# Waits of TensorE in the first attention, and the order of work in the mixture's front

## The chip, the cores and the metric

One core of a Trainium2 chip runs the whole program as one launch. Its engines work side by side and meet at semaphores: TensorE (PE, with its weight loads as PEld) multiplies, VectorE (DVE) and ScalarE (ACT) work on rows in SBUF and PSUM, GpSimd (POOL) and SyncE (SP) mostly issue transfers. The metric is the device time of one execution in microseconds, as the median of several runs. Before the change it is 1716.51 us (three runs, 1713.88 to 1717.43).

## What is computed

Two layers on 16 batches of 112 tokens of 256 features (1792 tokens), with a context of 375 rows for each batch:

```python
x = x + tanh(g_xattn[0]) * L0_xattn(layernorm(x), ctx)   # 16 heads of 64
x = x + tanh(g_ffn[0]) * L0_ffn(layernorm(x))            # quantised gate, up, down
x = x + tanh(g_xattn[1]) * L1_xattn(layernorm(x), ctx)   # 16 heads of 16, mask
x = x + tanh(g_ffn[1]) * L1_ffn(layernorm(x))            # mixture
# L1_ffn
normed = h * rsqrt(mean(h * h) + 1e-8) * norm_weight
shared = relu(normed @ sw1 + sb1) @ sw2 + sb2
probs = sigmoid(normed @ router_w.T)                     # 8 experts, the best 2
y = shared + sum over the 2 experts of weight * (relu(normed @ ew1 + eb1) @ ew2 + eb2)
```

## The kernel before

The kernel is written engine by engine: each phase is a block with one stream of instructions for each engine, in the order in which the Python code issues them, and `wait_ge(semaphore, value)` holds an engine's stream until a counter has reached a value. A block ends when all engines have reached its end. Every fp32 operand is split into a high and a low half in fp16, and a product is three matmuls (`products`, lines 294 to 296): ScalarE writes the high half, VectorE subtracts it and writes the low half.

**First attention** (`attention0_phase`). A slot g is one pair of heads of one batch; 8 slots are a batch, 128 slots in all. In slot g TensorE computes the scores of g (L505), the transposes of the probabilities of g-1 (L515), the first job of the slot, the weighted values of g-2 (to `a_ps_o`), and the rest of the jobs. Jobs are projections that later slots need: K, Q and V of a batch, the transposed output OT and the output product W. Their order is the table `JOBS`; `NUMBER` gives the place of a job in that sequence, and VectorE counts finished jobs in `job_lo`. A job may start when the job two places before it is finished (two PSUM banks), so that TensorE has by then waited for every value of `job_lo` up to that. ScalarE counts exponentials in `exp_done`, VectorE the low halves of the transposed probabilities in `pt_lo`, and the normalised outputs in `o_ready`. `scores(g)` waits for `job_lo` and for both exponentials of g-1; `transposes(g-1)` then waits again for those exponentials, one by one.

**Second attention** (`attention1_phase`) has slots of the same kind. In its last four slots (128 to 131) VectorE has only the last normalisation (`normalise`), the low half of the output (L1325) and the addition of W to the residual (L1333), each waiting for TensorE or ScalarE. SyncE stores each batch's residual to `out` (`kept`), the last one at L1127. After that block `clear_semaphores` runs, a short block of its own.

**The mixture's front** (`moe_front_phase`) begins with the statistics of the 16 batches (L1762, 16 instructions on VectorE), their aggregation, two square roots on ScalarE (L1689, L1691) with Newton steps on VectorE (`reciprocal_root`, L1753 to 1757), in between the halves of the router's weights and of the bias b2 (L1771, L1779). Then VectorE normalises batches 0 to 7 (L1788) and ScalarE 8 to 15 (L1696). The batches form four groups of four. TensorE transposes a group (L1570), ScalarE and VectorE split it (`high_x` L1671, `low_x` L1722), and `up(n)` is one step of the shared expert's first product (8 steps for each group, 32 in all). After the transposes come the router's logits (`route`, L1580 to 1583). Then TensorE alternates `up(n)` and `second(n-3)`, the second product into `m_p` (L1641; at a group's last step with the weighted biases, L1645), while VectorE works through routing: ranks, positions, the placement matrices (L1872, L1877, L1881). At a group's first step `second` waits tile by tile for `add`, in which VectorE adds the finished group to `y` (L1734) and so frees the PSUM. VectorE's order at a step n is `low(n)`, then at n = 11, 19 and 27 `add` of the group before; `low(n)` waits for ScalarE's half of step n (L1681).

**The routed experts** (`routed_experts_phase`) work through 35 tiles of 128 rows. TensorE first loads five packed words with the experts' numbers into registers (L1956), transposes tile 0 (L1970), ScalarE and VectorE split it (L2022, L2055), and then the products begin (L294, L1993). The tiles' rows are gathered by GpSimd; the first three gathers are issued in the front.

## Time and profile before

| what | value |
|---|---|
| median of three runs | 1716.51 us (1713.88 to 1717.43) |
| the profiled execution | 1717.06 us |
| its span, from the first instruction to the last | 1715.3 us |
| TensorE busy | 1420.7 us, 83% of the span |
| VectorE busy | 1235.3 us, 72% |
| ScalarE busy | 1116.1 us, 65% |
| GpSimd busy | 214.6 us, 13% |
| mean granted clock of TensorE | 0.917 of 2.4 GHz |

Busy times overlap between engines, so they don't add up to the span. A row of the timeline is a run of equal instructions on an engine; in square brackets stands how long the engine was idle before it and what ended that. A row that is an average over a stage says little about an edit; the rows further down are taken from the places that the diff touches.

### The profile page before, as it was taken

To read this page: it belongs to the slowest core of one execution; us is meant where nothing else is said; L and a number is where in the kernel's file an instruction comes from. 1 tells how busy PE (TensorE), PEld (TensorE's weight loads), DVE (VectorE), ACT (ScalarE), POOL (GpSimd) and SP (SyncE) were. 2 spreads that over 40 slices of the span, in tenths; PEclk is the share of its full clock that TensorE was granted. 3 is DMA by queue.
4 is the path that set the end of the run, shared out by engine and by line. 5 is a ranking of instruction groups with operands and counts; after the bars stand their busy time and mean duration, and the time that the engine had idled before them with its cause. 6 is when DMAs were issued, how large, how long until landed. Compare 5 with 4: busy or idle time off the path is not lost. (4 is left out here: it accounts for less than half of the span.)

```text
span 1715.3 us, 40917 instructions
## 1 busy us (share of the span) xinstructions
PE 1420.7 (83%) x15436; PEld 1010.6 (59%) x15436; DVE 1235.3 (72%) x3086; ACT 1116.1 (65%) x2453; POOL 214.6 (13%) x189
## 2 busy tenths in 40 slices
PE   1799999999999992680638898989889588899996
PEld 1467666766666762440625566566666366678884
DVE  6478888788788777678656898989888675334443
ACT  5467777777777763375236888888888452356663
POOL 4400000001000001200041000000000000034443
PEclk9999999999999997795857999999999588999998
DMA  4123232233222211000021121211100162112221
GB/s 143 52 69 109 83 96 90 81 105 95 97 93 93 72 56 56 1 0 0 1 78 40 49 82 42 82 42 33 33 17 11 32 226 63 47 30 45 48 49 23
DMA packets 64912, 105.72 MB, mean 62 GB/s; under 512 B 7433, under 2 KB 38898, under 8 KB 63570
## 3 DMA queue, kind: packets, MB, share of 16 engines
q1 hardware_dynamic: 58002, 94.83, 17.5%
q0 software_dynamic: 6720, 8.27, 2.9%
q8 instruction: 130, 2.13, 0.5%
q14 instruction: 60, 0.49, 0.1%
HBM read 68.88 MB, written 35.11 MB: 61 GB/s over the span
## 5 line engine op out<-in xcount | busy, mean ns | idle before, releaser
L1272 ACT ACTIVATE a_p<-a_s,a_nb 112x375 f32<-112x375 f32 x256 | 140.9, 598 | 26.2 <-DVE a_nb L1373 25.3
L294 PE MATMUL a_ps_o<-a_vh,a_pt 125*128 125x64 f16 (+1 forms) x1536 | 153.2, 183 | 3.0 <-ACT a_pt L1285 0.8
L1197 PE MATMUL a_ps_t<-ident,a_p 112*128 112x112 f32 x768 | 119.4, 288 | 40.0 <-ACT a_p L1272 39.5
L296 PE MATMUL a_ps_o<-a_vh,a_pt 125*128 125x64 f16 (+1 forms) x1536 | 151.3, 182 | 0.0
L295 PE MATMUL a_ps_o<-a_vl,a_pt 125*128 125x64 f16 (+1 forms) x1536 | 151.2, 182 | 0.0
L584 ACT ACTIVATE a_pt<-a_ps_t 125x336 f16<-125x336 f32 x256 | 102.7, 448 | 68.6 <-PE a_ps_t L515 68.0
L576 ACT ACTIVATE a_p<-a_ps_s,a_nb 112x375 f32<-112x375 f32 x256 | 143.8, 573 | 3.3 <-DVE a_scaled L667 3.3
L294 PEld LDWEIGHTS a_ps_o<-a_vh,a_pt 125*128 125x128 f16 x1536 | 133.8, 98 | 15.7 <-ACT a_pt L1285 7.4
L1364 DVE TENSOR_TENSOR a_s<-a_ps_s,a_mask 112x750 f32<-112x750 f32 x128 | 119.8, 936 | 26.2 <-PE a_ps_s L1187 21.1
L295 PEld LDWEIGHTS a_ps_o<-a_vl,a_pt 125*128 125x128 f16 x1536 | 131.2, 98 | 11.3
L1197 PEld LDWEIGHTS a_ps_t<-ident,a_p 112*128 112x128 f32 x768 | 81.4, 148 | 94.6 <-issue 80.1
L1373 DVE CUSTOM_DVE_ANT_0 a_s<-a_s,a_fill 112x375 f32<-112x375 f32 x256 | 129.9, 545 | 5.5
L667 DVE TENSOR_SCALAR_CACHE_REDUCE a_scaled<-a_ps_s 112x375 f32<-112x375 f32 x256 | 129.1, 542 | 5.7 <-POOL x_res L620 4.5
L2029 ACT ACTIVATE e_h<-e_p,tile_b 128x128 f32<-128x128 f32 x280 | 86.7, 366 | 68.1 <-PE e_p L296 68.1
L296 PEld LDWEIGHTS a_ps_o<-a_vh,a_pt 125*128 125x128 f16 x1536 | 129.4, 97 | 0.0
L2061 DVE TENSOR_TENSOR e_hl<-e_h,e_hh 128x512 f16<-128x512 f32 x70 | 48.5, 692 | 101.7 <-ACT e_hh L2036 101.7
L673 DVE TENSOR_TENSOR a_pt<-a_ps_t,a_pt 125x336 f16<-125x336 f32 x256 | 116.7, 497 | 1.1 <-ACT a_pt L584 1.0
L294 PE MATMUL a_ps_j<-a_cx,a_wk 128*128 128x375 f16 x320 | 105.9, 331 | 14.0 <-POOL a_neg L1309 10.4
L294 PE MATMUL a_ps_j<-a_wv,a_cx 128*125 128x512 f16 (+1 forms) x384 | 111.0, 308 | 2.6 <-DVE a_kl L1325 1.3
L294 PE MATMUL e_p<-e_xth,w1h 128*128 128x128 f16 x560 | 109.4, 220 | 1.9 <-DVE e_xtl L2055 1.6
L296 PE MATMUL a_ps_j<-a_wv,a_cx 128*125 128x512 f16 (+1 forms) x384 | 109.6, 304 | 0.0
L295 PE MATMUL a_ps_j<-a_wv,a_cx 128*125 128x512 f16 (+1 forms) x384 | 109.6, 304 | 0.0
(360 smaller groups left out, 4553.7 us busy)
## 6 DMA issues: line engine op xcount, KB each, us to landing
a_piece<-in_w SPq DMA_DIRECT2D x72, 256.0 KB, 3.1
split_weights<-a_pair SPq DMA_DIRECT2D x72, 256.0 KB, 3.4
w<-split_weights SPq DMA_DIRECT2D x8, 1024.0 KB, 6.1
a_ctx<-in_ctxT SPq DMA_DIRECT2D x16, 375.0 KB, 3.6
ctx<-a_cx SPq DMA_DIRECT2D x16, 375.0 KB, 4.3
a_cx<-ctx SPq DMA_DIRECT2D x16, 375.0 KB, 5.2
w1h<-split_weights SPq DMA_DIRECT2D x2, 1792.0 KB, 14.0
w1l<-split_weights SPq DMA_DIRECT2D x2, 1792.0 KB, 16.6
```

The costliest lines, as they stand in the source:

```text
L294: nc.tensor.matmul(out, wh, mh, start=(i == 0), stop=False)
L295: nc.tensor.matmul(out, wh, ml, start=False, stop=False)
L296: last = nc.tensor.matmul(out, wl, mh, start=False, stop=(i == n - 1))
L576: nc.scalar.activation(p32[:, g % 2, i, 0:NC], ps_s[0:S, i, 0:NC], ACT.Exp, bias=nb[:, g % 2, i:i + 1], scale=SC, accum_out=rsum[:, h:h + ...
L584: nc.scalar.activation(pt[:, g % 2, i, 0, :, 0:S], ps_t[0:KV, i, 0:NKV * S].rearrange("p (t s) -> p t s", t=NKV), ACT.Copy).then_inc(pt_hi, 1)
L667: nc.vector.tensor_scalar(scaled[:, i, :], ps_s[0:S, i, 0:NC], -SC, None, ALU.mult, ALU.min, accum_out=nb[:, g % 2, i:i + 1]).then_inc(max ...
L673: nc.vector.tensor_tensor(pt[:, g % 2, i, 1, :, 0:S], ps_t[0:KV, i, 0:NKV * S].rearrange("p (t s) -> p t s", t=NKV), pt[:, g % 2, i, 0, :, ...
L1197: mm = nc.tensor.matmul(ps_t[:, 2 * (g % 2) + i, t * S:(t + 1) * S], p32[:, g % 2, i, t * KV:t * KV + 128], ident32[0:S, 0:S], start=(t == ...
L1272: nc.scalar.activation(p32[:, g % 2, i, 0:NC], s2[:, g % 2, i, :], ACT.Exp, bias=nb[:, g % 2, i:i + 1], scale=-1.0).then_inc(exp_done, 1)
L1364: nc.vector.tensor_tensor(s1[:, r], ps_s[0:S, :, 0:NC], maskt[:, b % 2:b % 2 + 1, :].to_broadcast([S, 2, NC]), ALU.mult).then_inc(masked, 1)
L1373: nc.vector.tensor_tensor_reduce(out=s2[:, r, i, :], in0=s1[:, r, i, :], in1=fill[:, r, i, :], scale=-SC, scalar=3.0e38, op0=ALU.add, op1= ...
L2029: nc.scalar.activation(h32[:, 2 * (i % 2) + c, (j % 4) * 128:(j % 4 + 1) * 128], p1[:, 2 * (i % 2) + c, (j % 4) * 128:(j % 4 + 1) * 128], ...
```

## The change

Five parts.

1. First attention, TensorE: a wait is issued only where its value is above what the stream has waited for already. `scores` keeps its wait on `job_lo` in slot 0 alone, `transposes` keeps its wait on `exp_done` in the last slot alone, `weighted_values` drops `o_ready` and keeps `job_lo` at one place, W keeps its wait for the last two batches. The waits on `exp_done` in `scores` and on `pt_lo` stay.
2. The statistics of the front move to VectorE's stream at the end of the second attention: five in each of the slots 128, 129 and 130, the last one after the last addition to the residual.
3. The head of the front: ScalarE takes the square roots first and the small weights after its normalisations; the low halves of the router's weights and of b2 move behind VectorE's second group. VectorE normalises groups 0 to 2 and ScalarE group 3 (before: two each). TensorE transposes group g before `up(g-1)` instead of `up(g)`.
4. Group changes: `add` stands ahead of `low` on VectorE.
5. The end of the front: the loads of the experts' numbers, the transposes of tile 0 and its split move from the routed experts' block into the end of the front's block; the PSUM tiles of the second block change places so that `e_px` keeps its banks.

```diff
-                if name == "W":
+                if name == "W" and NUMBER["OT1", b] + 1 > i - 1:
                     pe.wait_ge(job_lo, NUMBER["OT1", b] + 1)
...
+            def taken_so_far(g, jobs_of_slot):
+                return len(FIRST) + sum(len(slot_jobs(j)) for j in range(g)) + jobs_of_slot - 2
+
             def scores(g):
                 b, p = divmod(g, NP)
-                pe.wait_ge(job_lo, max(NUMBER[f"K{p}", b], NUMBER[f"Q{p // 4}", b]) + 1)
+                needed = max(NUMBER[f"K{p}", b], NUMBER[f"Q{p // 4}", b]) + 1
+                if needed > taken_so_far(g, 0):
+                    pe.wait_ge(job_lo, needed)
                 wait(pe, exp_done, 2 * g)
...
             def transposes(g):
                 for i in range(2):
-                    pe.wait_ge(exp_done, 2 * g + i + 1)
+                    if g == G - 1:
+                        pe.wait_ge(exp_done, 2 * g + i + 1)
                     wait(pe, pt_lo, 2 * (g - 1) + i + 1)
...
-                    if h == 0:
-                        pe.wait_ge(job_lo, NUMBER["V02", b] + 1)
-                        wait(pe, o_ready, 2 * b - 1)
-                    if h == 8:
-                        pe.wait_ge(job_lo, NUMBER["V12", b] + 1)
-                        wait(pe, o_ready, 2 * b)
+                    if h in (0, 8):
+                        needed = NUMBER["V02" if h == 0 else "V12", b] + 1
+                        if needed > taken_so_far(g + 2, len(slot_jobs(g + 2)[:1])):
+                            pe.wait_ge(job_lo, needed)
```

The second attention's end, on VectorE:

```diff
                 if 0 <= g - 2 < G and (g - 2) % NP == NP - 1:
                     normalise((g - 2) // NP)
+                if g == G:
+                    dve.wait_ge(job_lo, NUMBER["W", B - 2] + 1)
+                if G <= g < G + 3:
+                    for t in range(5 * (g - G), 5 * (g - G) + 5):
+                        nc.vector.bn_stats(stats[:, t, :], x_res[:, t, :])
+            dve.wait_ge(job_lo, NUMBER["W", B - 1] + 1)
+            nc.vector.bn_stats(stats[:, B - 1, :], x_res[:, B - 1, :])
```

The front, TensorE, ScalarE and VectorE:

```diff
             for g in range(NG):
                 transpose(g)
-                if g < NG - 1:
-                    up(g)
+                if g > 0:
+                    up(g - 1)
             route()
...
+            pe.wait_ge(experts_ready, 1)
+            for n in range(NPACK):
+                experts.append(pe.snap(pe.value_load(tile_expert[0:1, n:n + 1], min_val=0, max_val=8 ** PACK - 1)))
+            pe.wait_ge(xt_in[0], 16)
+            pe.wait_ge(index_ready, 1)
+            for k in range(KD):
+                mm = nc.tensor.transpose(px[:, 0, k * 128:(k + 1) * 128], xt32[:, 0, k * 128:(k + 1) * 128], ident32[:])
+            mm.then_inc(tile_transposed, 1)
...
-            for t in range(HALF, B):
+            for t in range(B - TG, B):
                 nc.scalar.activation(norm[:, t, 0:D], norm[:, t, 0:D], ACT.Identity, bias=small[:, 7, t:t + 1],
                                      scale=small[:, 6, t:t + 1]).then_inc(normed_act, 1)
-                if t % 4 == 3:
-                    high_x(t // 4 - 2)
...
+            high_x(0)
+            high_x(1)
+            hidden(0)
             high_x(2)
-            hidden(0)
+            hidden(1)
             high_x(3)
-            hidden(1)
...
+            act.wait_ge(tile_transposed, 1)
+            nc.scalar.activation(xth[:, 0, :], px[:, 0, 0:D], ACT.Copy).then_inc(tile_hi, 1)
...
-            for t in range(B):
-                last = nc.vector.bn_stats(stats[:, t, :], norm[:, t, 0:D])
             stat(last)
...
-            for t in range(HALF):
-                nc.vector.tensor_scalar(norm[:, t, 0:D], norm[:, t, 0:D], mv[:, t, 0:1], small[:, 6, t:t + 1],
-                                        ALU.subtract, ALU.mult).then_inc(normed, 1)
-            low_x(0)
-            low_x(1)
+            for g in range(NG - 1):
+                for t in range(g * TG, g * TG + TG):
+                    nc.vector.tensor_scalar(norm[:, t, 0:D], norm[:, t, 0:D], mv[:, t, 0:1], small[:, 6, t:t + 1],
+                                            ALU.subtract, ALU.mult).then_inc(normed, 1)
+                if g > 0:
+                    low_x(g - 1)
+                if g == 1:
+                    dve.wait_ge(nw_ready, 1)
+                    dve.wait_ge(rw_hi, KD)
...
             for n in range(10, STEPS + LAG + 1):
+                if n % HC1 == LAG and n > LAG:
+                    add(n // HC1 - 1)
                 if n < STEPS:
                     low(n)
-                if n % HC1 == LAG and n > LAG:
-                    add(n // HC1 - 1)
...
+            dve.wait_ge(tile_hi, 1)
+            nc.vector.tensor_tensor(xtl[:, 0, :], px[:, 0, 0:D], xth[:, 0, :], ALU.subtract).then_inc(tile_lo, 1)
```

## Rows read from the trace of the kernel before

**Rows 1.** Windows: us, busy us (instructions) of each engine, granted clock, transfers
```profile
core 0: us, PE busy (x) PEld busy (x) DVE busy (x) ACT busy (x) POOL busy (x), PEclk, DMA share, GB/s
...
1388.20:1495.60 107.40, 98.92 (x720) 73.26 (x720) 59.76 (x179) 40.05 (x67) 3.20 (x3) 0.92 0.28 89
```

**Rows 2.** Waits of TensorE after 1360 us: total, times, longest in us
```profile
PE e_px L1970 <- issue: 7.0, 1, 7.0
PE m_p L1641 <- DVE m_y L1734: 5.0, 2, 2.5
PE m_p L1641 <- DVE x_res L1734: 2.5, 1, 2.5
```

**Rows 3.** Timeline, first attention: start, duration, engine; then its separate waits by source
```profile
253.05 0.21 ACT L576 ACTIVATION_READ_ACCUMULATOR a_p<-a_ps_s,a_nb 112x1 f32 x1
253.38 0.12 PEld L505 LDWEIGHTS a_ps_s<-a_kh,a_qh 64*128 64x128 f16 x2 [0.46 <-DVE a_vl L648]
...
256.75 0.69 DVE L648 TENSOR_TENSOR a_vl<-a_ps_j,a_vh 125x512 f16<-125x512 f32 x1 [0.49 <-ACT a_vh L560]
257.50 0.10 PEld L294 LDWEIGHTS a_ps_j<-a_cx,a_wk 128*128 128x128 f16 x1 [0.31 <-DVE a_vl L648]
257.62 0.21 ACT L576 ACTIVATION_READ_ACCUMULATOR a_p<-a_ps_s,a_nb 112x1 f32 x1
258.56 0.10 PEld L505 LDWEIGHTS a_ps_s<-a_kh,a_qh 64*128 64x128 f16 x2 [0.31 <-issue]
...
L52 PEldq EVENT_SEMAPHORE  x354: 51/51/51, 142.4 to 641.0; - x177
```

**Rows 4.** Timeline, end of the second attention and head of the front
```profile
1357.38 0.58 DVE L1325 SCALAR_TENSOR_TENSOR a_otl<-a_ps_j,a_bias,a_oth 128x112 f16<-128x112 f32 x2 [1.42 <-ACT a_oth L1265]
1359.58 0.48 DVE L1333 SCALAR_TENSOR_TENSOR x_res<-a_ps_j,a_gate,x_res 112x256 f32<-112x256 f32 x1 [1.62 <-PE a_ps_j L296]
1360.09 0.32 SPq L1127 DMA_DIRECT2D out_x<-x_res  x1
1362.13 5.33 DVE L1762 BATCH_NORM_STATS2 m_stats<-x_res 112x6 f32<-112x256 f32 x16
1365.84 1.28 ACT L1689 ACT_TABLE_LOAD   x1
1370.96 0.22 ACT L1691 ACTIVATE m_small<-m_small 112x16 f32<-112x16 f32 x1 [1.85 <-DVE m_small L1777]
1371.86 0.23 DVE L1753 RECIPROCAL m_small<-m_small 112x16 f32<-112x16 f32 x1
1373.31 2.67 DVE L1788 TENSOR_SCALAR x_res<-x_res,m_mv,m_small 112x256 f32<-112x256 f32 x8
1373.42 2.08 ACT L1696 ACTIVATE x_res<-x_res,m_small 112x256 f32<-112x256 f32 x4 [1.94 <-DVE m_small L1784]
```

**Rows 5.** Timeline of TensorE from the first transposes to routing
```profile
1374.74 1.75 PE L1570 MATMUL m_p<-ident,x_res 112*128 112x112 f32 x8 [15.20 <-DVE x_res L1788]
1377.79 0.55 PE L294 MATMUL m_p<-xh,w1h 128*128 128x448 f16 x1 [1.29 <-DVE xl L1722]
...
1380.00 1.43 PE L1570 MATMUL m_p<-ident,x_res 112*128 112x112 f32 x8
...
1388.23 0.19 PE L1580 MATMUL m_px<-m_rw,xh 128*112 128x16 f16 x1 [1.53 <-DVE xl L1722]
```

**Rows 6.** Timeline of VectorE at the first group change
```profile
1416.52 2.55 DVE L1877 TENSOR_TENSOR x_res<-x_res,m_part 112x1120 f16<-112x1120 f16 x2
...
1421.16 1.65 DVE L1734 SCALAR_TENSOR_TENSOR m_y<-m_p,m_gate,m_y 112x256 f32<-112x256 f32 x4
```

**Rows 7.** Windows of the front with TensorE's clock at 0.50, columns as above
```profile
1422.00:1425.30 3.30, 3.30 (x16) 2.54 (x15) 2.04 (x4) 0.00 (x0) 0.00 (x0) 0.50 0.44 127
1445.90:1456.10 10.20, 7.65 (x27) 4.63 (x27) 3.22 (x7) 1.35 (x3) 0.00 (x0) 0.50 0.16 47
```

**Rows 8.** Loads of the experts' numbers by source, and the first routed product
```profile
L1956 PEldq TENSOR_LOAD <-tile_expert x5: 295/309/1421, 1498.2 to 1502.0; - x5
...
1504.40 0.28 PE L294 MATMUL e_p<-e_xth,w1h 128*128 128x128 f16 x1 [1.09 <-DVE e_xtl L2055]
```

More of the change, by code:

```diff
@@ L1467, in moe_front_phase @@
          rows_out, numbered, shared_in, w1_in, up_done, relu_done,
-         h_hi, h_lo, down_done, bias_chain, added, gate_made) = (sem(f"m_{n}") for n in names)
+         h_hi, h_lo, down_done, bias_chain, added, gate_made, experts_ready) = (sem(f"m_{n}") for n in names)
         y_in = [sem(f"m_y_in{i}") for i in range(2)]
+        experts, xth, xtl, tile_transposed, tile_hi, tile_lo = first_tile
         NSMALL = 16 * 4
@@ L1767, in _ @@
             nc.vector.tensor_scalar(var, mv[:, :, 1], 1e-5, None, ALU.add).then_inc(var_ready, 1)
-            dve.wait_ge(nw_ready, 1)
-            dve.wait_ge(rw_hi, KD)
-            for k in range(KD):
-                last = nc.vector.scalar_tensor_tensor(out=rw[:, k, 1, :], in0=rw32[:, k, :], scalar=nws[:, k:k + 1],
-                                                      in1=rw[:, k, 0, :], op0=ALU.mult, op1=ALU.subtract)
-            last.then_inc(rw_ready, 1)
             reciprocal_root(var, std, rstd, 1)
@@ L1924, in _, with routed_experts_phase @@
                     bias(nc.vector.tensor_reduce(tile_b1[:, :, j], bsel, AX.X, ALU.add))
-def routed_experts_phase(nc, w1, w2, tile_expert, tile_b1, pick, share, target, xt32, xt_in, rows, out, stored, ident32):
+            dve.wait_ge(tile_hi, 1)
+            nc.vector.tensor_tensor(xtl[:, 0, :], px[:, 0, 0:D], xth[:, 0, :], ALU.subtract).then_inc(tile_lo, 1)
+def routed_experts_phase(nc, w1, w2, tile_expert, tile_b1, pick, share, target, xt32, xt_in, rows, out, stored, ident32,
+                         first_tile):
     HR, YR = 3, 3
@@ L1955, in _ @@
         def _(pe):
-            experts = [pe.snap(pe.value_load(tile_expert[0:1, n:n + 1], min_val=0, max_val=8 ** PACK - 1))
-                       for n in range(NPACK)]
             w1f = [[w1[part][k][:].rearrange("p e n -> p (e n)") for k in range(KD)] for part in range(2)]
@@ L2121, in moe_phase @@
         xt_in = [sem(f"tile_x_in{i}") for i in range(XR)]
+        xth, xtl = sb("tile_xh", [128, 2, D], F16), sb("tile_xl", [128, 2, D], F16)
+        first_tile = ([], xth, xtl, *(sem(f"tile_{n}") for n in ("x_transposed", "x_hi", "x_lo")))
         w1 = [[sb(f"w1{part}{k}", [128, E, FF1], F16) for k in range(KD)] for part in ("h", "l")]
         moe_front_phase(nc, A, x_all, xh, xl, ident32, tanh_g, split_w, w1, w2s, w2_in, tile_expert, tile_b1, pick, share,
-                        target, xt32, xt_in, rows, out, kept, y, stored)
-        routed_experts_phase(nc, w1, w2, tile_expert, tile_b1, pick, share, target, xt32, xt_in, rows, out, stored, ident32)
+                        target, xt32, xt_in, rows, out, kept, y, stored, stats, first_tile)
+        routed_experts_phase(nc, w1, w2, tile_expert, tile_b1, pick, share, target, xt32, xt_in, rows, out, stored, ident32,
+                             first_tile)
 def program(nc, A, out):
```

72 lines of the change are left out of this document (37 added, 35 removed).

## The prediction

> **What bounds the kernel now.** I read the profile in this order: the stretches, to see which engine runs without a break; the waits of TensorE, to see where it does stop; then the timelines at those places, because only there can an edit of order pay. In the mixture's front from 1388.2 to 1495.6 us TensorE is busy 98.92 of 107.4 us, the other engines 60 us and less [rows 1]: it is the bound, so time is won there only by closing its idle gaps. The waits list them [rows 2]: three waits of 2.5 us for the additions of line 1734, and one of 7.0 us at the routed experts' first transposes, put down to "issue". The longest, 15.2 us, stands before the first transposes of the front [rows 5]. There the bound is a serial chain on VectorE, not TensorE. In the first attention (about 54 to 657 us) TensorE's stream is nearly unbroken as well, with only short pauses at the scores.
>
> **Part 1, waits of TensorE in the first attention.** By counting jobs, the edit drops about 456 waits on values that the same queue has passed already: 127 before scores, 254 before transposes, 61 before weighted values (31 on `job_lo`, 30 on `o_ready`), 14 before W. A wait beyond the one which an instruction carries is an instruction of 51 ns [rows 3]. Where the value is there long before, I cost it at nothing: for the weights load at 258.56 the exponential was over at 257.83, and the pause before it is put down to issue. The same pause stands before every group of scores or transposes, whichever waits it has, and I leave it standing. Where the value comes last, it costs: the exponential ends at 253.26 and the weights load at 253.38, 0.12 us later, through the extra instruction. A weight load that carries its one wait itself started at 257.50, 0.06 us after VectorE's 256.75 + 0.69 [rows 3]. So each late value is worth 0.06 us. Of eight slots, three have scores that wait for the exponential (after V01, V11, and K2), and a fourth has transposes that wait for VectorE behind W. ScalarE's exponential there comes after a job that TensorE itself made, so a gain is passed on round the loop. 16 batches x 4 x 0.06 = 3.8 us. Bounds: 0 if another queue holds the loop; 6 us if that issue pause shrinks at some slots too.
>
> The Trainium skill ("TensorE: Matmul & The Clock Gate", section "Architectural detail") says that TensorE's queue can pull weight loads ahead of matmuls in flight. By that alone dropped waits are worth nothing, and the sum would be 3.8 us less; that is the first rival below.
>
> **Part 2, the head of the front.** 16 statistics instructions, 5.33 us [rows 4], leave the chain between the last residual and the normalisation. 15 of them go into the end of the second attention. Five run while VectorE waits for the last weighted values. Five come after the last `normalise`: VectorE is free 1.42 us before 1357.38, so they end at 1355.96 + 5 x 0.333 = 1357.63, and the low half of the output, which starts at 1357.38 now [rows 4], starts 0.25 us later. Five follow that low half and end at about 1359.93, just when the last W (1359.58 + 0.25) is due: 0.35 us later in all. Queued behind them is only W's addition, for which SyncE waits with its store. The 16th takes 0.41 us behind W; SyncE's store at 1360.09 takes 0.32 us [rows 4] and its drain more, so this one is covered; uncovered it would cost 0.4. In the chain, VectorE's low half of b2 goes: ScalarE's root is ready at 1370.96 + 0.22, but the next reciprocal starts at 1371.86 [rows 4], so 0.65 us go. Normalisation starts at 1373.31 - 5.33 - 0.65 + 0.35 = 1367.7, 5.6 us earlier. Normalisation waits for the store of batch 15 too, but that is issued 7 us ahead of it. The root needs its table loaded: 1.28 us [rows 4], from about 1362.2, and the root is due at 1364.0, so it is covered.
>
> The page "ScalarE: Activation LUTs" of the Trainium skill (section "What ACT_TABLE_LOAD costs") adds a drain of about 1.38 us to each load. With it the load would end near 1364.9, and the head would be 0.9 us longer; no row here shows that drain, since the root now waits for VectorE anyway.
>
> Then the chain from normalisation (1373.31) to routing (1388.23) is 14.9 us [rows 4, 5]. After: VectorE normalises groups 0 to 2 (1.33 us each, from 2.67 for eight), ScalarE only the last four (2.08 us) [rows 4]. TensorE transposes group 0 from +1.4 and group 1 behind it, 1.75 us each at 1.2 GHz [rows 5], to +4.9. From the first transposes to the first `up` now pass 3.05 us (1374.74 to 1377.79); I add 0.7 for ScalarE's small weights, which stand ahead of the high halves then: +5.15. That `up` takes 2.2 us at 1.2 GHz (1377.79 to 1380.00) [rows 5], to +7.35. VectorE's third group (+7.2) is ready for it. From there at 2.4 GHz, half of each: transposes 0.9, `up` 1.1, transposes 0.9, `up` 1.1, and 1.1 in all for waits on ScalarE's and VectorE's halves (now 1.29 us before the first `up` and 1.53 before routing [rows 5]): routing at +12.5. That is 2.4 us less, with 1 us either way for the moment when the clock rises. SyncE's fetch of group 0 waits for b2, 1.6 us later than now, and behind it in its queue are the stores of the rows and the large weight loads; the stores wait for normalised rows anyway, and TensorE waits for none of these transfers. The shared weights, which the first `up` needs at 1372.8, are issued from 1363.6 to 1365.1 and now used at 1377.79; they are the one transfer that could take the cover away, up to 1 us. Part 2: 5.6 + 2.4 = 8.0 us; bounds 6 and 9.
>
> **Part 3, group changes.** `add` before `low`. Now `low(11)` waits for ScalarE and holds `add(0)` back until 1421.16 [rows 6], so TensorE idles 2.48 us. VectorE is free at 1416.52 + 2.55 = 1419.07, so the first tile is added at 1419.55 and the matmuls start 0.3 us after 1419.3; the additions come every 0.39 us against 0.33 us of matmuls, another 0.2. Gain 2.0. At the other two changes VectorE is idle, the additions start when the group's last matmul ends and are done 1.65 us later, while TensorE does an `up` of 1.1 us and takes the tiles one by one: no wait left, 2.5 + 2.5. What waits behind `add` is `low`, and it needs ScalarE's half, 1.2 us after the `up` ends: covered. 7.0 us. The granted clock is at 1.2 GHz from 1422.0 to 1425.3, right after the first gap, and from 1445.9 to 1456.1 around the second [rows 7]. Work there takes twice as long. Without the gaps I give 2 us back of the 5 which those stretches cost beyond the gaps. Part 3: 9.0; bounds 5.5 and 12.
>
> **Part 4, the end of the front.** Five loads of the experts' numbers take 1498.2 to about 1502.5 [rows 8], the first 1.42 us, then transposes and both halves, and `up` starts at 1504.40. After: the loads follow the last matmul (about 1495.2) and end at 1499.6, beside VectorE's last additions (to 1497.3); transposes 0.68, ScalarE 0.38, VectorE 0.43 end at 1501.2; the block's end takes 0.4 and the register work 0.3, `up` at 1501.9: 2.5 us. Bounds 1.5 and 3.
>
> **Sum.** 3.8 + 8.0 + 9.0 + 2.5 = 23.3 us. The profiled execution took 1717.06 us, so 1693.8; the median of the runs shown is 0.55 us under it, which makes 1693.
>
> **Rivals.**
> *The dropped waits are worth nothing* in the first attention, because TensorE's queue has read them ahead: 1697. For it: most of the waits are covered [rows 3]. Against: the 0.12 us at 253.38.
> *The gaps at the group changes close but the clock stays as it is*, or VectorE's placements hold the first one: part 3 is 5.5, 1697. For it: the stretch from 1445.9 begins before the second gap [rows 7]. *The table's drain* adds 0.9: 1694.
> *More than forecast*: with a dense stream the front has no stretch at 1.2 GHz after 1381 and part 1 reaches its bound: 1687.
> *Slower*: TensorE's clock. After the new head and the closed gaps the front might be granted 1.2 GHz where it now has 2.4. At 0.5 against 1.0 its stream takes twice the time, so 23 us are gone when 46 us of the 107 us in [rows 1] run so; twice that gives 1740. Against it: low stretches stand behind gaps, and the gaps go.
> *The change doesn't do what it says*: the dropped waits weren't separate instructions, or the compiler puts them back: that is within the first rival.
>
> **How the numbers follow.** Forecast 0.62, first rival 0.15, second with the drain 0.12, more 0.05, slower 0.03, others 0.03. The likeliest gives 1693. Lower end: 6 + 9 + 12 + 3 = 30 us, 1687. Upper: 0 + 6 + 5.5 + 1.5 = 13 us, 1704. A measurement of this kernel tells 0.2% (3.4 us) from no change: every case but slower and others is past it. Faster 0.94, same 0.02, slower 0.04.
>
> **What would show it.** TensorE's wait at line 1570 falls from 15.2 to about 9.5 us; the waits on line 1734's additions fall to under 1 us in all; "issue" before the routed experts is gone and the first `up` comes about 6.3 us after the last matmul of the front, against 8.8 (1495.6 to 1504.4); the distance between the scores of two batches in the first attention falls by 0.24 us. If the latter is unchanged, part 1 is wrong; if PEclk shows the same low stretches in the front, the clock's share of part 3 is.

## The result

The changed kernel takes 1686.85 us (median of four runs, 1684.1 to 1687.35), the kernel before 1715.71 us in the same comparison (four runs, 1713.88 to 1717.43). The ratio is 0.9825, with a 95% interval from 0.9812 to 0.9839: 30.0 us less by the ratio, between 27.6 and 32.3 (the two medians differ by 28.9). The prediction was 1693 us, 23.3 us less, with a range from 1687 to 1704. So the direction was right, the gain too small, and the time lies 0.15 us below the range. All these runs are fast ones; of the runs further down one is slow (1976.59 us at a mean clock of 0.715, one of twelve of the kernel with part 1 alone), and the ratios leave it out.

The profiled execution of the changed kernel took 1687.02 us, its span is 1685.3 us. Cut at five events that both traces have, the 30.0 us between the two spans are:

| stretch | before | after | gain | forecast |
|---|---|---|---|---|
| start to the last residual of the second attention (VectorE's row on L1333, now L1340) | 1360.06 | 1356.28 | 3.8 | 3.8 - 0.35 |
| last residual to the first normalisation | 13.25 | 8.61 | 4.6 | 5.95 |
| first normalisation to routing | 14.92 | 11.85 | 3.1 | 2.4 |
| routing to the last matmul of the front | 107.38 | 94.52 | 12.9 | 9.0 |
| last matmul of the front to the first routed `up` | 8.79 | 3.05 | 5.7 | 2.5 |
| first routed `up` to the end | 210.9 | 211.0 | -0.1 | 0 |

Two terms are far off: the stretch behind routing gained 3.9 us more than forecast and the end of the front 3.2 us more. The head gained 1.3 us less.

The stretch behind routing in the changed kernel, as the windows show it (us, busy us and count of TensorE, its weight loads, VectorE, ScalarE and GpSimd, granted clock, share of the transfers' engines, GB/s); it answers [rows 1]:

```profile
1376.74:1471.26 94.52, 93.25 (x720) 70.69 (x720) 59.90 (x179) 38.80 (x66) 3.20 (x3) 0.98 0.39 130
```

The same 720 matmuls as in [rows 1] are busy for 93.25 us instead of 98.92, at a mean clock of 0.98 instead of 0.92, and the idle time is 1.3 us instead of 8.5. Closing the gaps gave 7.2 us, the clock the other 5.7.

TensorE's waits in the changed kernel from 1355 us on (total, times, longest), against [rows 2, 5]:

```profile
PE m_p L1584 <- DVE x_res L1802: 10.7, 2, 10.6
PE e_p L294 <- PEq L1429: 1.4, 1, 1.4
PE m_px L1684 <- issue: 1.2, 1, 1.2
PE m_px L1594 <- DVE xl L1746: 1.1, 1, 1.1
PE m_px L1615 <- DVE m_wT L1764: 0.9, 1, 0.9
PE m_p L1655 <- DVE m_y L1758: 0.3, 1, 0.3
```

The wait for the first transposes fell from 15.2 to 10.6 us (forecast: about 9.5). Of 7.5 us of waits for the additions 0.3 are left. The 7.0 us of "issue" at the routed experts' first transposes became 1.2 us (L1684) and 1.4 us at the block's end.

### The profile page after: what moved, and what is told of

It is laid out like the page before. It is cut to its first block and busy times, and to the rows that moved or that the text cites. A ratio compares the mean times of both kernels' runs of the same rounds, so it can differ in the third digit from the quotient of the medians.

```text
span 1685.3 us, 40493 instructions
## 1 busy us (share of the span) xinstructions
PE 1414.1 (84%) x15436; PEld 1006.3 (60%) x15436; DVE 1234.5 (73%) x3090; ACT 1110.6 (66%) x2449; POOL 214.3 (13%) x189
## 5 line engine op out<-in xcount | busy, mean ns | idle before, releaser
L295 PEld LDWEIGHTS a_ps_o<-a_vl,a_pt 125*128 125x128 f16 x1536 | 131.1, 98 | 11.2 <-issue 0.3
L294 PE MATMUL a_ps_j<-a_wv,a_cx 128*125 128x512 f16 (+1 forms) x384 | 112.5, 310 | 2.6 <-DVE a_kl L1332 1.3
L294 PE MATMUL e_p<-tile_xh,w1h 128*128 128x128 f16 x560 | 110.2, 222 | 2.0 <-PEq L1429 1.4
L296 PE MATMUL a_ps_j<-a_wv,a_cx 128*125 128x512 f16 (+1 forms) x384 | 111.2, 307 | 0.0
L295 PE MATMUL a_ps_j<-a_wv,a_cx 128*125 128x512 f16 (+1 forms) x384 | 111.1, 307 | 0.0
```

The costliest lines, as they stand in the source:

```text
L294: nc.tensor.matmul(out, wh, mh, start=(i == 0), stop=False)
L295: nc.tensor.matmul(out, wh, ml, start=False, stop=False)
L296: last = nc.tensor.matmul(out, wl, mh, start=False, stop=(i == n - 1))
```

## The parts one by one

Four kernels take one part of the change each; their times go against the kernel before (the parts of the prediction; part 3 is the order of `add` and `low`, part 4 the end of the front). They tell whether the parts add up and where each term of the sum stands.

### Part 1 alone

```diff
-                pe.wait_ge(job_lo, max(NUMBER[f"K{p}", b], NUMBER[f"Q{p // 4}", b]) + 1)
+                needed = max(NUMBER[f"K{p}", b], NUMBER[f"Q{p // 4}", b]) + 1
+                if needed > taken_so_far(g, 0):
+                    pe.wait_ge(job_lo, needed)
...
-                    pe.wait_ge(exp_done, 2 * g + i + 1)
+                    if g == G - 1:
+                        pe.wait_ge(exp_done, 2 * g + i + 1)
```

and the other edits of part 1.

> The kernel before with part 1 alone (the dropped waits of the first attention). Theory: five places in each batch move. The scores of slots 1, 5 and 6 start 0.09 us sooner each, the transposes behind W 0.155 us sooner, and the transposed output of slot 6 gives 0.095 us back because it waits for VectorE anyway: the distance of two batches falls from 36.98 to 36.73 us and the time by 3.9 us (ratio 0.9977). Rival: the gain seen at the end of the first attention is lost again in the phases behind it, because their low stretches of the clock lie elsewhere: then less than 2 us are left (ratio above 0.9988).

Measured: 1712.55 us, ratio 0.9973 [0.9963, 0.9984], a gain of 2.7 to 6.4 us. The distance of two batches is 36.74 us, where it was 36.98. The 3.8 us of the forecast hold, and they are not lost again.

Here is one of the three places where the exponential comes last. First three rows of the timeline of the kernel before, then the same three of the changed one (start, duration, engine, line; idle time before it and its releaser):

```profile
290.04 0.21 ACT L576 ACTIVATION_READ_ACCUMULATOR a_p<-a_ps_s,a_nb 112x1 f32 x1
290.36 0.12 PEld L505 LDWEIGHTS a_ps_s<-a_kh,a_qh 64*128 64x128 f16 x2 [0.46 <-DVE a_vl L648]
290.39 0.34 PE L505 MATMUL a_ps_s<-a_kh,a_qh 64*128 64x375 f16 x2
```

```profile
288.61 0.21 ACT L583 ACTIVATION_READ_ACCUMULATOR a_p<-a_ps_s,a_nb 112x1 f32 x1
288.87 0.10 PEld L511 LDWEIGHTS a_ps_s<-a_kh,a_qh 64*128 64x128 f16 x2 [0.40 <-ACT a_p L583]
288.87 0.33 PE L511 MATMUL a_ps_s<-a_kh,a_qh 64*128 64x375 f16 x2
```

The accumulator's row ends at 290.25 and the weights load 0.11 us later; in the changed kernel it ends at 288.82 and the weights load 0.05 us later. That is the 0.06 us of the prediction. But the matmul gains 0.09 us, since it started 0.03 us behind its weight load and now starts with it. The wait that was named before was VectorE's `a_vl`, the last semaphore in the record; now it is the exponential, which is what the prediction had argued.

The 0.24 us of a batch are made up of five places, found by laying TensorE's matmuls of a batch of both traces side by side: scores of slots 1, 5 and 6 0.09 us each, the transposes behind W 0.065 us, and at the transposed output of slot 6 (L477) 0.093 us are given back. There the kernel waits for VectorE's normalised output, which depends on weighted values that no dropped wait brings forward.

### One kind of wait alone

The first kernel drops `job_lo` ahead of the scores only:

> The kernel before with the waits on job_lo dropped ahead of the scores alone (the other dropped waits of part 1 stay in). Theory: the scores of slots 1, 5 and 6 start 0.09 us sooner each, because the exponential comes last there and one wait instead of two stands between it and the first weight load; the gain of slot 6 is given back at the transposed output. The distance of two batches falls by 0.18 us, from 36.98 to 36.80. The transposes behind W stay. Rival (the queue reads waits ahead, so their number doesn't matter): 36.98.

Measured: 36.80 us between two batches. The three scores start 0.087 us sooner each, the transposed output gives 0.093 back, and the transposes behind W stay where they were. The theory holds.

The second kernel drops only the waits that have been met long before:

```diff
-                    if h == 0:
-                        pe.wait_ge(job_lo, NUMBER["V02", b] + 1)
-                        wait(pe, o_ready, 2 * b - 1)
...
-                if name == "W":
+                if name == "W" and NUMBER["OT1", b] + 1 > i - 1:
                     pe.wait_ge(job_lo, NUMBER["OT1", b] + 1)
```

> The kernel before with only those waits dropped that stand ahead of the weighted values (job_lo, o_ready) and of W. Their values are there long before at every one of these places. Theory: nothing, the distance of two batches stays at 36.98 us within 0.01. Rival (each dropped instruction gives its 51 ns back): 0.05 us for each, with five of them in a batch 36.73 us.

Measured: 36.98 us, and none of the 406 matmuls of a batch shifted by more than 0.015 us against the kernel before. The edit drops five waits of a batch, but only two of them were instructions of their own: of 389 separate waits of 51 ns between 100 and 650 us 357 are left (272 in the kernel with the scores' waits dropped, 2 in the changed one). So the rival's price is 0.10 us a batch and not 0.25, and even that is not there. In the kernel with part 1 alone the 26 separate waits of a batch are all gone, and only four places gain. A wait that is met in advance costs nothing, though it is an instruction of 51 ns; one that stands between a late value and the work that needs it costs its time and a bit more. Both sentences were in the prediction, and the sum was right, 4 x 0.06 = 0.24. That it was right to 0.01 us is luck: three places give 0.09 and one 0.065, and one of the four gains is handed back, while the prediction had all four passed on.

### Part 2 alone

The edits of part 2 and 3 of the change's list, of which the largest on VectorE is:

```diff
-            for t in range(B):
-                last = nc.vector.bn_stats(stats[:, t, :], norm[:, t, 0:D])
             stat(last)
             for t in range(B):
                 last = nc.vector.bn_aggr(mv[:, t, :], stats[:, t, :])
```

> The kernel before with part 2 alone (the statistics in the second attention, the new head). Theory: 4.6 us from the last residual to the first normalisation and 3.1 us from there to routing, 7.7 us (ratio 0.9955); the low stretches behind routing stay as before, since the gaps at the group changes are there still. Rival of the clock: they go with the new head, and the kernel gains 13 us (ratio 0.992).

Measured: 1707.87 us, ratio 0.9948 [0.9935, 0.9960], 6.9 to 11.2 us. In the trace: last residual 1361.66, normalisation 1370.27 (8.61 us), routing 1382.12 (11.85 us), the same two distances as in the changed kernel, so 7.7 us. The three gaps of 2.5 us at the group changes are there, and so are stretches at 1.2 GHz behind the first two of them. They are the 3.40 us windows here, with a clock of 0.50; the gaps were 1413.2 to 1415.7 and 1441.2 to 1443.7:

```profile
1416.90:1420.30 3.40, 3.40 (x14) 2.07 (x14) 1.05 (x1) 0.45 (x1) 0.00 (x0) 0.50 0.47 135
1444.20:1447.60 3.40, 3.40 (x15) 2.22 (x13) 1.57 (x4) 0.00 (x0) 0.00 (x0) 0.50 0.49 140
```

The statistics in the second attention delay its end by 0.12 us (last scores to last residual: 12.75 us before, 12.86 here), not by 0.35.

### Part 3 alone

```diff
             for n in range(10, STEPS + LAG + 1):
+                if n % HC1 == LAG and n > LAG:
+                    add(n // HC1 - 1)
                 if n < STEPS:
                     low(n)
-                if n % HC1 == LAG and n > LAG:
-                    add(n // HC1 - 1)
```

> The kernel before with part 3 alone (add before low). Theory: the low stretches of the clock at 1422 and 1446 us are caused by the gaps at the group changes, and go with them. Then the front gains the gaps, 7.2 us, and 5.5 us of clock: 12.7 us (ratio 0.9926). Rival: the clock in the front is set by how the front begins (its head and when it starts); then this kernel gains 7.2 us only (ratio 0.9958) and the stretches at 1.2 GHz between 1400 and 1490 us stay at 10 us or more.

Measured: 1706.46 us, ratio 0.9940 [0.9926, 0.9955], 7.7 to 12.7 us. The window from routing to the last matmul:

```profile
1385.55:1480.07 94.52, 93.26 (x720) 70.44 (x720) 59.91 (x179) 39.95 (x67) 3.20 (x3) 0.98 0.31 99
```

94.52 us, as in the changed kernel, with the head as it was. So both the gaps and the low stretches went with the order of `add` and `low`, and part 3 alone gives the 12.9 us of these traces. Each trace is one execution; the six times, with 7.7 to 12.7 us, would also allow a gain little over the gaps' 7.2. Of the first gap 0.31 us is left (forecast: 0.5), of the others nothing.

### The gap put back

The changed kernel with `low` ahead of `add` again at the second change:

```diff
-                if n % HC1 == LAG and n > LAG:
+                if n % HC1 == LAG and n > LAG and n // HC1 != 2:
                     add(n // HC1 - 1)
                 if n < STEPS:
                     low(n)
+                if n % HC1 == LAG and n // HC1 == 2:
+                    add(1)
```

> The changed kernel with add behind low again at the second group change only. Theory (a gap of 2.5 us brings a stretch at 1.2 GHz behind it): the gap of 2.5 us is back there, a stretch of 3.4 to 10.2 us at 1.2 GHz begins within 4 us of it, and the front is 2.5 + 1.7 to 2.5 + 5.1 us longer (4.2 to 7.6). Rival (the clock doesn't follow this gap): 2.5 us, and no stretch between 1400 and 1470 us.

Measured: the gap is 2.55 us, from 1428.48 to 1431.03, and the front takes 102.47 us from routing, 7.95 more than 94.52. The windows of the front and of the low stretch:

```profile
1370.76:1473.23 102.47, 98.65 (x720) 73.85 (x720) 59.84 (x179) 38.94 (x66) 3.20 (x3) 0.92 0.37 120
1426.60:1436.80 10.20, 7.65 (x29) 4.93 (x27) 3.21 (x7) 1.89 (x4) 0.00 (x0) 0.50 0.20 51
```

TensorE is busy for 98.65 us instead of 93.25. Of these 5.4 us the low stretch at the gap makes 3.8 (7.65 us busy at half the clock). The rest, 1.6, has nothing to do with the gap: the stretch at 1.2 GHz right behind routing is 6.8 us long here and 3.4 us in the changed kernel. Two kernels without gaps also have 6.8 us there (loads held back and GpSimd's memsets moved, in the table below), and their fronts take 96.06 and 96.04 us. Here is the first of them, its front and its stretch:

```profile
1371.59:1467.65 96.06, 94.80 (x720) 71.78 (x720) 59.91 (x179) 38.91 (x66) 3.20 (x3) 0.96 0.38 126
1373.40:1380.20 6.80, 6.80 (x47) 5.53 (x47) 3.75 (x21) 2.62 (x5) 0.00 (x0) 0.50 1.01 356
```

Against them the gap of 2.55 us costs 6.4 us: itself and 3.8 us at 1.2 GHz. But the low stretch begins at 1426.6, 1.9 us ahead of the gap, and 55.8 us behind routing. With no gap at all, the kernel with the second statistics (below) had a stretch of 3.4 us at 55.7 us behind its routing. So at this place the clock may fall by itself; the gap makes it 10.2 us long. What lets it fall there was not found.

All executions profiled, by the number of gaps of 2.5 us (routing to the last matmul of the front; us at 1.2 GHz more than 20 us behind routing, and us at 1.2 GHz in the stretch right behind routing). All of them also have a pause of 0.95 us some 21 us behind routing.

| kernel | gaps | us | at 1.2 GHz, later | right behind routing |
|---|---|---|---|---|
| before | 3 | 107.38 | 13.7 | 3.4 |
| part 1 alone | 3 | 108.23 | 6.8 | 10.2 |
| scores' waits alone | 3 | 107.38 | 13.7 | 3.4 |
| covered waits alone | 3 | 106.99 | 10.2 | 3.4 |
| part 2 alone | 3 | 105.43 | 6.8 | 3.4 |
| part 4 alone | 3 | 108.57 | 6.8 | 10.2 |
| gap put back | 1 | 102.47 | 10.2 | 6.8 |
| changed | 0 | 94.52 | 0 | 3.4 |
| part 3 alone | 0 | 94.52 | 0 | 3.4 |
| loads held back | 0 | 96.06 | 0 | 6.8 |
| loads spread | 0 | 94.52 | 0 | 3.4 |
| statistics twice | 0 | 97.70 | 3.4 | 6.8 |
| digits' memsets moved | 0 | 94.51 | 0 | 3.4 |
| GpSimd's memsets moved | 0 | 96.04 | 0 | 6.8 |

The means are 107.3 with three gaps and 95.4 with none: 11.9 us, of which 7.2 are the gaps. The rest, 4.7 us, is the clock. Of it 0.4 us is the stretch right behind routing, which every execution has and which makes most of the scatter within a group (5.7 against 4.9 us long in the mean, and half of a stretch is lost); 4.3 us are left for the later stretches, where the prediction gave 2. The six kernels with three gaps have 18 gaps and 12 later stretches: ten begin in a gap or at most 1.3 us behind its end, two begin 2.5 us ahead of one, and six gaps have none. So the low stretches keep to the gaps, but not every gap brings one.

### Part 4 alone

The kernel before with point 5 of the change's list:

```diff
-            experts = [pe.snap(pe.value_load(tile_expert[0:1, n:n + 1], min_val=0, max_val=8 ** PACK - 1))
-                       for n in range(NPACK)]
...
-            transpose(0)
```

in the second block, and the same work at the end of the first.

> The kernel before with part 4 alone (loads of the experts' numbers and tile 0 in the front's end). Theory: TensorE's sequencer reads the five loads while its last matmuls are still queued, the first of them about 2.4 us before the last matmul ends; the first routed product comes 3.1 us after the last matmul of the front, against 8.8 before: 5.7 us less (ratio 0.9967). Rival, my prediction's step: the loads start when the last matmul ends, the first routed product comes 6.3 us after it, and 2.5 us go (ratio 0.9985).

Measured: 1709.37 us, ratio 0.9956 [0.9940, 0.9972], 4.8 to 10.3 us. From the last matmul of the front (1495.39) to the first routed `up` (1498.71) pass 3.32 us, against 8.79: 5.5 us. The five loads in the changed kernel (durations shortest, median and longest in ns; first and last start):

```profile
L1680 PEldq TENSOR_LOAD <-tile_expert x5: 301/310/489, 1468.9 to 1471.7; - x5
```

The last matmul of the front ends at 1471.26, and the first load starts at 1468.9, 2.4 us ahead of it: the sequencer had by then handed on every matmul and was free. So the loads end 1.0 us behind the last matmul, not 4.0 as in the prediction. That could have been read in the kernel before, at the end of the block. DRAIN is the sequencer's wait for the engine to finish:

```profile
L1415 PEldq DRAIN  x1: 2410/2410/2410, 1493.2 to 1493.2; - x1
```

It starts at 1493.2 and the last matmul ends at 1495.6. The Trainium skill ("TensorE: Matmul & The Clock Gate", the table at its head) gives TensorE a queue of 64 entries. The trace doesn't contradict it: behind the start of the first load 14 matmuls and 14 weight loads still start.

### The loads held back

The changed kernel, with one line more ahead of the loads:

```diff
             pe.wait_ge(experts_ready, 1)
+            pe.wait_ge(down_done, STEPS)
             for n in range(NPACK):
```

> The changed kernel with one wait more: TensorE loads the experts' numbers only after its own last matmul of the front has been counted, which is where the prediction had put them. Theory (the sequencer runs ahead of the matmuls): the five loads take 3.4 us from there, and the first routed product comes 5.5 to 6.3 us after the last matmul of the front, against 3.05. Rival (the loads are short wherever they stand, and the gain was the end of the block): still about 3.1.

Measured: 1688.7 us, ratio 0.9839 [0.9807, 0.9870], too wide to say anything on 3 us. In the trace, one execution, the last matmul ends at 1467.65 and the first routed `up` starts at 1474.18: 6.5 us instead of 3.05.

```profile
L1681 PEldq TENSOR_LOAD <-tile_expert x5: 309/494/801, 1467.8 to 1470.9; - x5
```

With the loads behind the last matmul, as the prediction had them, the end takes 6.5 us; the prediction said 6.3. The place of the loads is worth 3.5 us, and the error of part 4 was 3.2.

The four ratios of the parts alone give 4.6, 8.9, 10.3 and 7.5 us, together 31.3, with intervals 4 to 6 us wide; the stretches between their events give 3.8, 7.7, 12.9 and 5.5, together 29.9. The change as a whole gives 30.0: the parts add up, and no interplay between them shows.

### The loads spread

```diff
                 if n == FIND_AT:
                     find()
-            pe.wait_ge(experts_ready, 1)
-            for n in range(NPACK):
-                experts.append(...)
+                k = n - (STEPS + LAG - 1 - NPACK)
+                if k == 0:
+                    pe.wait_ge(experts_ready, 1)
+                if 0 <= k < NPACK:
+                    experts.append(...)
```

> The changed kernel with the five loads spread over the last steps of the front, one behind each step's second product, ahead of the last step. Theory: a load takes the sequencer 0.67 us of a step of 2.45 us and it is 2.4 us ahead, so no gap appears among the matmuls, and the pause of 1.2 us before the transposes of tile 0 shrinks to 0.2: the first routed product comes 2.0 us after the last matmul of the front, 1.0 us sooner than with the change. Rival: each load stops the matmuls for its 0.3 us or more; then the front is 1.5 to 3 us longer and the kernel no faster than the changed one.

Measured: 1685.69 us, ratio 0.9820 [0.9800, 0.9841], not to be told from the changed kernel. The front is 94.52 us long again, so the loads stop no matmul. The pause ahead of the transposes is gone, but only 0.3 us of the 1.0 arrive: the first routed `up` comes 2.8 us after the last matmul of the front. The timeline shows what is next late:

```profile
1471.04 0.44 PE L1686 MATMUL m_px<-ident,x_res 128*128 128x128 f32 x2
1471.15 1.66 DVE L1760 SCALAR_TENSOR_TENSOR x_res<-m_p,m_gate,x_res 112x256 f32<-112x256 f32 x4 [5.59 <-PE m_p L1659]
1471.52 0.38 ACT L1740 ACTIVATE tile_xh<-m_px 128x256 f16<-128x256 f32 x1 [6.62 <-PE m_px L1686]
1472.73 0.41 DVE L1953 TENSOR_TENSOR tile_xl<-m_px,tile_xh 128x256 f16<-128x256 f32 x1
1473.89 0.10 PEld L294 LDWEIGHTS e_p<-tile_xh,w1h 128*128 x1 [2.64 <-issue]
```

ScalarE's half is ready at 1471.90, but VectorE is in its last additions until 1472.81, and only then splits the tile and ends the block. The expectation had looked at TensorE alone.

## The head: a wrong theory that was confirmed twice

The head gained 4.6 us instead of 5.95. Its rows in the changed kernel, against [rows 4]:

```profile
1358.16 0.18 DVE L1784 MEMSET m_digit<- 1x5 f32 x5 [1.42 <-PEq L83]
1358.66 0.09 DVE L1784 MEMSET m_digit<- 1x5 f32 x2 [0.32 <-issue]
1358.79 1.17 DVE L1787 BATCH_NORM_AGGREGATE m_mv<-moe_stats 112x2 f32<-112x6 f32 x16
1359.99 0.64 DVE L1789 TENSOR_SCALAR m_small<-m_mv 112x16 f32<-112x16 f32 x1
1361.20 0.19 DVE L1778 TENSOR_TENSOR m_tmp<-m_small 112x16 f32<-112x16 f32 x1
1361.64 0.55 DVE L1780 TENSOR_SCALAR m_tmp<-m_tmp 112x16 f32<-112x16 f32 x1
1364.89 2.67 DVE L1802 TENSOR_SCALAR x_res<-x_res,m_mv,m_small 112x256 f32<-112x256 f32 x8
```

The memsets pause for 0.32 us, and two additions of 16 elements take 0.64 and 0.55 us, where the same instructions took 0.17 and 0.18 us before. My first theory: VectorE's instructions arrive late at the head of a block, and the 5.33 us of statistics had given them time. The changed kernel gets the statistics a second time, ahead of the aggregation:

```diff
             stat(last)
+            for t in range(B):
+                last = nc.vector.bn_stats(stats[:, t, :], norm[:, t, 0:D])
+            stat(last)
             for t in range(B):
                 last = nc.vector.bn_aggr(mv[:, t, :], stats[:, t, :])
```

> The changed kernel with the 16 statistics instructions done a second time at the head of the front, as the kernel before has them there: 5.3 us of VectorE ahead of the aggregation. In the change, VectorE's memsets at the head pause for 0.32 us, and two small instructions of the chain take 0.64 and 0.55 us, where their like take 0.17 and 0.18 before. Theory (the first instructions of a block come late for VectorE, and the long instructions gave the fetch time): both are back to 0.17 and 0.18, and from the aggregation to the first normalisation 5.2 us pass instead of 6.1. Rival (something else at this place in the chain is slow, such as ScalarE's or the transfers' use of memory): 6.1 stays.

Measured: from the aggregation (1358.32) to the first normalisation (1363.59) 5.27 us, the two additions at 0.17 and 0.18 us. The pause at the memsets stayed. Then the memsets were moved:

```diff
-            for i in range(PACK):
-                last = nc.vector.memset(digit[:, i:MAXT:PACK], float(8 ** i))
-            stat(last)
...
             low_x(3)
+            for i in range(PACK):
+                last = nc.vector.memset(digit[:, i:MAXT:PACK], float(8 ** i))
+            bias(last)
```

> The changed kernel with the seven memsets of the experts' digits taken out of the head of the front and put behind the last low_x. Theory (VectorE's instructions arrive late at the head of the block, whatever they are): the 0.63 us from the first memset to the aggregation go only in part, since the pause moves on to the aggregation or the small instructions behind it; from VectorE's first instruction of the block to the first normalisation 6.4 us pass or more, against 6.73. Rival (the pause belongs to the memsets): 6.10 us.

Measured: 6.76 us from VectorE's first instruction (1356.39) to the first normalisation (1363.15), so nothing is gained, as the theory said. It was wrong all the same. In this trace one of the two additions had grown to 1.12 us, which late instructions could explain as well as anything. What explains the number is another engine's rows, here VectorE and GpSimd of this kernel side by side:

```profile
1357.27 1.58 POOL L1558 MEMSET m_wT<- 9x1792 f16 x1
1357.76 1.12 DVE L1786 TENSOR_SCALAR m_small<-m_mv 112x16 f32<-112x16 f32 x1
1358.80 1.61 POOL L1559 MEMSET m_wT<- 9x1792 f16 x1
1359.90 0.55 DVE L1780 TENSOR_SCALAR m_tmp<-m_tmp 112x16 f32<-112x16 f32 x1
```

The addition starts at 1357.76 and ends at 1358.88, GpSimd's memset ends at 1358.85; the second ends at 1360.45, the second memset at 1360.41. The statistics had only kept VectorE off the additions until GpSimd was done. The test takes GpSimd's memsets away from the head of the kernel just shown (the digits' memsets are moved as there, and the loads are spread):

```diff
-            nc.gpsimd.memset(wT[:, 1], 0.0).then_inc(consts, 1)
-            nc.gpsimd.memset(wT[:, 0], 1.0).then_inc(consts, 1)
...
+            pool.wait_ge(normed, TG * (NG - 1))
+            nc.gpsimd.memset(wT[:, 1], 0.0).then_inc(consts, 1)
+            nc.gpsimd.memset(wT[:, 0], 1.0).then_inc(consts, 1)
```

> The changed kernel with the loads spread (as in e6), the digits' memsets behind low_x (as in e8), and GpSimd's two long memsets of the weights' tile, 1.6 us each, held back until VectorE has normalised its three groups. New theory of the head: the slow instructions of VectorE there are no late fetch; each ends with a memset of GpSimd (in the changed kernel 1359.99 + 0.64 = 1360.63 against 1359.02 + 1.58 = 1360.60, and 1361.64 + 0.55 = 1362.19 against 1360.55 + 1.61 = 1362.16), so VectorE waits for GpSimd. Then both are back to 0.17 and 0.18 us and 5.3 us pass from the aggregation to the first normalisation, against 6.10, and 5.3 us from VectorE's first instruction of the block, against 6.73. Old theory (instructions arrive late at the head of a block): the pauses stay, 6.7 us from VectorE's first instruction, as with the digits' memsets moved alone. In all the new theory gives 1.7 us less than the changed kernel, from 1.4 at the head and 0.3 at the end: a ratio of about 0.981 to the kernel before.

```profile
1360.01 1.33 DVE L1787 BATCH_NORM_AGGREGATE m_mv<-moe_stats 112x2 f32<-112x6 f32 x16 [1.40 <-PEq L83]
1361.38 0.17 DVE L1789 TENSOR_SCALAR m_small<-m_mv 112x16 f32<-112x16 f32 x1
1362.56 0.18 DVE L1783 TENSOR_SCALAR m_tmp<-m_tmp 112x16 f32<-112x16 f32 x1
1365.44 2.67 DVE L1802 TENSOR_SCALAR x_res<-x_res,m_mv,m_small 112x256 f32<-112x256 f32 x8
```

5.43 us from VectorE's first instruction to the normalisation, where the old theory had 6.7. The two additions are back to 0.17 and 0.18 us: VectorE waited for GpSimd. The Trainium skill says it ("SBUF — State Buffer", section "Who interferes with whom"): a `tensor_scalar` in a two-port mode and a GpSimd instruction can't hold the shared pair of ports at once, and the later one waits in full; a `tensor_tensor` is not held up by a GpSimd instruction that only writes. The trace agrees with both: the TENSOR_TENSOR at 1361.20 in the changed kernel runs under GpSimd's second memset (1360.55 to 1362.16) in its 0.19 us. Whether the additions run in a two-port mode no row shows. The pause of 0.32 us at the digits' memsets ends with GpSimd's select (1358.39 + 0.29), which would be the same thing, but was not tried by itself. So of the 1.3 us that the head lacks 0.84 are shown to be GpSimd's (0.64 and 0.55 us instead of 0.17 and 0.18); the other 0.45 stand at the digits' memsets, which delay the aggregation by 0.63 us instead of 0.18, and their cause is argued only.

In time nothing came of it: 1687.34 us, ratio 0.9835 [0.9815, 0.9855], against 0.9825 for the changed kernel. TensorE's wait at the head fell by 1.3 us to 9.25, but in the profiled execution the stretch at 1.2 GHz behind routing was 6.8 us long instead of 3.4, and the front took 96.04 us instead of 94.52. No kernel tried is shown to beat the changed one.

## Why the prediction came out as it did

- **What bounds it**: right. In the front TensorE is the bound, and the gain came from its idle gaps, its head and its end.
- **Part 1**, 3.8 us: right in sum, by two errors that cancel (0.09 us at the scores instead of 0.06, and one gain given back). The first rival, that TensorE's queue reads waits ahead and they are worth nothing, fell: waits met in advance are worth nothing, but the others, which the sum counted, are worth what it said.
- **Part 2**, 8.0 us: 7.7 in the trace, so near only because errors cancel. The head lost 1.3 us, of which 0.84 at least to GpSimd, which the prediction didn't look at; the chain to routing took 11.85 us instead of 12.5, and the second attention's end was delayed by 0.12 us instead of 0.35. That GpSimd works at the head stood in the trace of the kernel before, under the statistics. The rival of the table's drain changed nothing: the load ends at 1359.39 (1358.11 + 1.28), and the root starts at 1360.67, 0.04 us after VectorE's addition, which was late by itself. That alone doesn't refute a drain of 1.38 us, but with GpSimd's memsets moved the root starts 0.34 us after the load's end (1361.25, 1361.59). And the trace of the kernel before could have struck out this rival, in the second attention's first exponential, where ScalarE waits for nothing:

```profile
913.97 0.57 ACT L1253 ACTIVATE a_kh<-a_ps_j,a_bias 128x375 f16<-128x375 f32 x1 [2.88 <-PE a_ps_j L296]
914.57 1.28 ACT L1272 ACT_TABLE_LOAD   x1
915.86 1.11 ACT L1272 ACTIVATE a_p<-a_s,a_nb 112x375 f32<-112x375 f32 x2
```

  The load follows the instruction before it after 0.03 us and the next one follows the load after 0.01 us: no drain shows on either side, and the load costs its 1.28 us.
- **Part 3**, 9.0 us: 12.9 in the two profiled executions, over its bound of 12; 11.9 in the means. The gaps were right (7.0 forecast, 7.2 measured); the step that failed is "without the gaps I give 2 us back of the 5". All of the low stretches behind the group changes went, and they were 13.7 us long. The doubt rested on the stretch from 1445.9, which begins before its gap; it was right that it does, and wrong that it would therefore stay: six of the seven executions without gaps have no stretch there, and the seventh has one of 3.4 us.
- **Part 4**, 2.5 us: 5.7. The step that failed is "the loads follow the last matmul (about 1495.2)": they start 2.4 us ahead of its end and are done 1.0 us behind it, not 4.0. The upper bound of 3 didn't contain it; with 5.7 in its place the lower end of the range would have been 1684.
- **The range** took the extremes of the terms as known. Its lower end, 30 us, was just met, because parts 3 and 4 went past their bounds while parts 1 and 2 stayed inside theirs; unrounded it is 1686.5 us (1716.51 - 30), so that the time misses it by the rounding alone. The bounds that broke were the 3 us of part 4, set without a row of its own, and the 12 of part 3.
- **More than forecast**, 1687: the time is this rival's, but its way only in part. The front has one short stretch at 1.2 GHz left, which is near what the rival says of the clock; part 1 stayed at 3.8 and did not reach its bound, and part 4, which the rival left alone, gave the rest.
- **Slower**, by the clock: the opposite happened.

The executions differ by some microseconds in stretches that no edit touched: from the last scores of the first attention to those of the second pass 692.0 to 699.2 us in the fourteen traces (698.1 before, 698.3 after), with the low stretches of the clock in other places each time. So a kernel's total is no measure for an edit of 1 us, but the distance between two events around it is.

## What to carry to other kernels

Time an edit between the two events next to it, and read at both of them what all engines do, not only the two that the edit names: both misses at the head and at the end of the front were rows of an engine or a sequencer that the prediction had not opened. Before a sequencer's own work (register loads, branches) is put behind matmuls, look how far it runs ahead of them: a block's DRAIN shows it, and that much is hidden. A gap in a dense stream of TensorE costs more than its length, since a stretch at 1.2 GHz often comes with it (at 12 of 18 gaps): here three gaps together cost 1.6 times their length in the mean (11.5 us for 7.2, without the stretch right behind routing), and the one put back two and a half times (6.4 us for 2.55, one execution).

## What the runs showed of the hardware

- TensorE's sequencer ran 2.4 us ahead of the last matmuls in the front, both before (DRAIN of 2410 ns) and after. Five loads of an SBUF word into registers, 0.3 to 0.5 us each, spread over five steps, stopped no matmul.
- The same load took 1421 ns as the first instruction of a block [rows 8], and 301 to 489 ns inside one; held back by a wait, 309 to 801 ns.
- A table load of ScalarE took 1.28 us, and the activation behind it started 0.01 us after its end.
- An instruction of 16 elements on VectorE took 1.12 us instead of 0.17 under a memset of GpSimd of 1.58 us.
- A wait between a late value and the weights load cost 0.06 us to the load and 0.09 us to the matmul; a wait met in advance cost nothing.
